# Batch one's front reworked, decays announced by halves, loads reordered: a gated SSM with a quantised FFN on one core

## The reference, cut to what matters

```
# Mamba-like mixer on ctx, gated by layernorm(x)
xin   = in_proj_w @ ctx ; xc = causal depthwise conv, 4 taps ; u = silu(xc + conv_b)     # 256 channels
dt, Bm, Cm = x_proj_w @ u                                      # 8 + 16 + 16 rows
delta = softplus(dt_proj_w @ dt + dt_proj_b) ; A = -exp(A_log)
state = state * exp(delta * A) + (delta * u) * Bm              # scan over 256 tokens, 16 states a channel
y = (sum_n state * Cm + D * u) * silu(layernorm(x))
x = x + tanh(g_xattn) * y
# FFN on layernorm(x): act_quant to 8 bits, ternary weights, gate/up 256 -> 1024,
# silu(gate) * up, Walsh-Hadamard transform, act_quant, ternary down 1024 -> 256
x = x + tanh(g_ffn) * ffn(layernorm(x))
```

## Time and profile before

| | before |
|---|---|
| median of three runs | 223.75 us |
| the profiled execution, its own time | 223.4 us |
| its span, first to last instruction | 221.6 us |
| DVE busy | 188.3 us (85%), 292 instructions |
| ACT busy | 172.8 us (78%), 302 instructions |
| PE busy | 167.9 us (76%), 1216 matmuls |
| POOL busy | 148.5 us (67%), 247 instructions |
| ACT table loads | 14 |
| granted TensorE clock, mean | 0.937 |
| first scan starts | 28.55 us |
| last product with C ends | 185.06 us |

### The profile page before, as it was taken

One profiled execution on the slowest core, in us unless ns is written; L12 is line 12 of the kernel. 1 busy time (PEld: TensorE's weight loads), 2 busy tenths in 40 slices (PEclk: granted clock), 3 DMA queues, 4 the chain that ended last, 5 costly groups with the idle time before them and its releaser, 6 DMA issues.

```text
span 221.6 us, 3745 instructions
## 1 busy us (share of the span) xinstructions
PE 167.9 (76%) x1216; PEld 136.7 (62%) x1216; DVE 188.3 (85%) x292; ACT 172.8 (78%) x302; POOL 148.5 (67%) x247
## 2 busy tenths in 40 slices
PE   2757475997897994979867968988587598677873
PEld 1535354796695984748757864877484487544751
DVE  3462889597999999999999899999979996889983
ACT  0699997799899989799879895999497630985373
POOL 1103039969787989999999999999995299510000
PEclk9965587579999999999999999999999999999999
DMA  4994000000000000000000000000000000000001
...
DMA packets 8148, 6.33 MB, mean 29 GB/s; under 512 B 2202, under 2 KB 7874, under 8 KB 8130
## 3 DMA queue, kind: packets, MB, share of 16 engines
...
...
## 4 chain that ended last, share of the span: by engine, by line
POOL 25%; DVE 11%; PE 11%; ACT 8%; issue 4%; POOLq 0%; DVEq 0%; ACTq 0%
POOL driveT L1413 7%; POOL wnat L1479 7%; POOL wnat L1478 7%; PE GP L601 2%; DVE wnat L1789 2%; ACT L1242 2%; PE PY L483 2%; PE BC L422 1%; DVE wnat L1792 1%; DVE wnat L1730 1%; DVE prod L1686 1%; DVE state L1609 1%; PE UP L422 1%; ACT xn L1163 1%; DVE wnat L1778 1%
## 5 line engine op out<-in xcount | busy, mean ns | idle before, releaser
L1413 POOL TENSOR_SCALAR driveT<-duT,BT 128x256 f32<-128x256 f32 x120 | 58.4, 506 | 14.6 <-ACT duT L1071 11.9
L1054 ACT ACTIVATE decay<-delta,zero_c,aneg 128x255 f32<-128x255 f32 x128 | 65.0, 588 | 0.1
L1686 DVE TENSOR_TENSOR prod<-state,BC 128x1024 f32<-128x1024 f32 x32 | 38.5, 1202 | 3.2 <-PE BC L467 2.7
L1609 DVE TENSOR_TENSOR_SCAN state<-decay,BC 128x512 f32<-128x512 f32 x30 | 36.4, 1212 | 2.0 <-ACT decay L1054 1.2
L1609 DVE TENSOR_TENSOR_SCAN state<-decay,UP 128x512 f32<-128x512 f32 x30 | 35.9, 1198 | 0.0
L483 PE MATMUL PY<-id,prod 128*128 128x128 f32 x256 | 33.0, 273 | 0.8 <-DVE prod L1686 0.5
L483 PEld LDWEIGHTS PY<-id,prod 128*128 128x128 f32 x256 | 28.7, 140 | 1.8 <-issue 0.8
L1478 POOL TENSOR_TENSOR wnat<-wnat 128x512 f32<-128x512 f32 x18 | 22.9, 1271 | 8.0 <-DVE wnat L1730 7.2
L422 PE MATMUL BC<-id,driveT 128*128 128x128 f32 x120 | 19.4, 286 | 8.2 <-POOL driveT L1413 4.4
L1479 POOL TENSOR_TENSOR wnat<-wnat 128x512 f32<-128x512 f32 x18 | 22.9, 1272 | 0.0
L422 PEld LDWEIGHTS BC<-id,driveT 128*128 128x128 f32 x120 | 14.4, 148 | 11.9 <-issue 5.5
...
## 6 DMA issues: line engine op xcount, KB each, us to landing
...
```

The lines of the kernel that those rows point to most:

```text
L1054: last = nc.scalar.activation(decay[:, m % RING, h, n, 1:L], delta[:, b % 2, h, 1:L], ACT.Exp, bias=zero_c[:], scale=aneg[:, h, NB * j + n ...
L1413: last = nc.gpsimd.tensor_scalar(driveT[:, m % RING, c, n], duT[:, b % 2, c], BT[:, b % 2, c, NB * j + n:NB * j + n + 1], 1.0, ALU.mult, A ...
L1609: nc.vector.tensor_tensor_scan(state[:, g % STATES, h].rearrange("p n l -> p (n l)"), decay[:, g % RING, h].rearrange("p n l -> p (n l)"), ...
L1686: nc.vector.tensor_tensor(prod[:, g % RING].rearrange("p h n l -> p h (n l)"), state[:, g % STATES].rearrange("p h n l -> p h (n l)"), PC. ...
```

## The change

1. **Loads.** The DMAs of `conv_b`, `dt_proj_w`, `dt_proj_b` and `D` move from SP's queue to ACT's (ACT issues 9 instead of 5 before it computes). On SP the rest moves up, and `x` (1 MB) is loaded ahead of the gate weights (1 MB).
2. **Early table.** `setup_loads` on ACT ends with a load of the silu set. The load at L994 and the `for_silu()` behind `first_tap` are gone.
3. **Bias in silu.** `first_tap` is a Copy with a scale; `conv_b` is added by the silu of batch 0, which becomes one activation for each half.
4. **Softplus in pieces.** `softplus(n)` is cut into `spread(n)` (Abs, and Relu from batch 1 on) and `softplus(n)` (Exp, Ln). For batch 0 DVE does the Relu (`first_relu`), and subtracts before the Ln is there (`first_rest`), so that one addition is left behind it (`first_delta`).
5. **Halved decays.** `decays(m)` becomes `decays(m, h)`, each with its own count; `scan(m, h)` waits for its half alone, and a half of a ring slot is written again once that half was scanned.
6. **New order** of the calls on PE, ACT, POOL and DVE, in the whole program.

```diff
@@ softplus_tail
-                    eng.wait_ge(act_decay, STEPS * (n - 1))
+                    eng.wait_ge(act_decay, HALF * STEPS * (n - 1))
@@ sync
-            sp.dma_start(cb[:], conv_b...)
             sp.dma_start(xpw[:], x_proj_w).then_inc(ld_small, 16)
-            sp.wait_ge(zeroed, 1)
-            sp.dma_start(dtw[:, :, DT0:DT0 + DR], dt_proj_w...)
-            for dst, src in ((dtb, dt_proj_b), (dskip, D)): sp.dma_start(dst[:], ...)
             sp.dma_start(ctxs[:, 1:B]...).then_inc(ld_ctx, 16)
+            sp.dma_start(xs[:]..., tiles(x)).then_inc(ld_x, 16)
             sp.dma_start(wnat[:, 0]..., w_gate...).then_inc(ld_w[0], 16)
-            sp.dma_start(xs[:]..., tiles(x)).then_inc(ld_x, 16)
@@ dt_proj
                 elif n == 1:
                     pe.wait_ge(act_spread, 1)
+                    pe.wait_ge(dve_relu, 1)
@@ scalar: setup_loads, first_tap
+                act.dma_start(cb[:], conv_b...) ; act.wait_ge(zeroed, 1) ; act.dma_start(dtw..., dt_proj_w...)
                 ... gates, gates, alog ...
+                act.dma_start(dtb ...) ; act.dma_start(dskip ...)
+                nc.scalar.preload_act_table_set("silu_and_others")
-                act.wait_ge(ld_cb, 16)
-                    last = nc.scalar.activation(conv[:, h], bank4[...], ACT.Identity, bias=cb[:, h:h + 1],
+                    last = nc.scalar.activation(conv[:, h], bank4[...], ACT.Copy,
                                                 scale=cw[:, h, DC - 1:DC])
@@ decays
-            def decays(m):
+            def decays(m, h):
                 if m >= RING:
-                    act.wait_ge(dve_scan, HALF * (m - RING + 1))
-                for h in range(HALF):
-                    for n in range(NB):
+                    act.wait_ge(dve_scan, HALF * (m - RING) + h + 1)
+                for n in range(NB):
@@ silu_u(0)
-                    nc.scalar.activation(u[:, 0], conv[:], ACT.Silu, bias=zero_c[:]).then_inc(act_u, 1)
+                    act.wait_ge(ld_cb, 16)
+                    for h in range(HALF):
+                        last = nc.scalar.activation(u[:, 0, h], conv[:, h], ACT.Silu, bias=cb[:, h:h + 1])
+                    last.then_inc(act_u, 1)
@@ spread, softplus
+            def spread(n):
                 act.wait_ge(pe_draw, n + 1)
                 ...
-                    nc.scalar.activation(spr[:, h], v, ACT.Relu, bias=dtb[:, h:h + 1])
+                    if n >= 1:
+                        nc.scalar.activation(spr[:, h], v, ACT.Relu, bias=dtb[:, h:h + 1])
                     last = nc.scalar.activation(spa[:, h], v, ACT.Abs, bias=dtb[:, h:h + 1])
                 last.then_inc(act_spread, 1)
+            def softplus(n): ... Exp, Ln as before
@@ vector
-                dve.wait_ge(act_decay, g + 1)
+                dve.wait_ge(act_decay, HALF * g + h + 1)
+            def first_relu():
+                dve.wait_ge(act_spread, 1)
+                dve.wait_ge(ld_conv, 16 * 2)
+                for h in range(HALF):
+                    last = nc.vector.tensor_scalar(spr[:, h], dt_bank(0)[:, L * h:L * (h + 1)], dtb[:, h:h + 1], 0.0,
+                                                   ALU.add, ALU.max)
+                last.then_inc(dve_relu, 1)
+            def first_rest():       # spm = (1 + spe) - 1 - spe on act_sp_link, then:
+                link(nc.vector.tensor_tensor(spm[:], spr[:], spm[:], ALU.subtract))
+            def first_delta():
+                dve.wait_ge(act_sp, 1)
+                nc.vector.tensor_tensor(delta[:, 0], spl[:], spm[:], ALU.add).then_inc(delta_ready, 1)
+                du_of(0, dve, nc.vector)
@@ scalar, the list of calls, its beginning now
             setup_loads() first_tap() tanh_gates() silu_u(0) xpw_out() dtw_out() for_exp() dt_rows(0)
             high_pieces(0) weight_abs(0) spread(0) inw_out() exp_A() softplus(0) copy_B(0) copy_BT(0)
             first_rstd() ctx_out() weight_abs(1) copy_B(1) decays(0, 0) decays(0, 1) decays(1, 0) decays(1, 1)
             copy_duT(0) for_silu() silu_u(1) silu_z(0) for_exp() decays(2, 0) dt_rows(1) copy_BT(1)
             high_pieces(1) decays(2, 1) spread(1) decays(3, 0) decays(3, 1) softplus(1) decays(4, 0) ...
```

497 lines of the change are left out of this document (267 added, 230 removed).

## The result

| | before | changed |
|---|---|---|
| median | 223.67 us (4 runs) | 226.65 us (225.87 to 228.56, 4 runs) |
| the profiled execution, its own time | 223.4 us | 225.87 us |
| its span | 221.6 us | 224.1 us |
| first decay | 26.45 us | 26.57 us |
| first scan | 28.55 us | 27.70 us |

What follows compares the result with a forecast made beforehand. Front bound by ACT, middle by DVE with POOL close behind, tail by a barely touched chain. 223.4 - 1.9 (front) - 1.0 (middle) = 220.5 us, with the median 0.35 above: 220.9 us, range 217.7 to 224.8.

Steps and rivals of the forecast that it cites:

- Loads, "Zero": Load order: new order and queues cost nothing; small loads took 2.7 us to land, alog needed at 8.5 us.
- which fits: ACT's start: some 4.5 us of issuing plus one table load get done before 7.46 us.
- both orders serve: Large loads: x has slack until 19.7 us, gate weights wanted at 15.7 us, so either may go first.
- The middle, "It just fits. I take 1.0 us": POOL's drives(21) ends at 125.6 us, needed at 126.7; 1.0 us gained from DVE's waits, ends 0 and 4.5.
- so it keeps the 1.9 us: Middle: DVE does the same work from times_C(4) on, so the 1.9 us gained by then stays.
- Rival (b): PE, step to batch 1: PE stays at half clock, front's gain lost, middle gives 0.5; 223.2 us, chance 0.22.
- Front: ACT up to first decay: 26.1 us against 26.45; first scan 27.1, times_C(4) 52.1 against 54.05.
- Halved decays: First scan waits for two activations, not four: 1.0 us saved; later in the run little.
- copy_duT(1): Copy that lets POOL start its chain: moved ahead of silu_z(1), to 60.2 us, 1.6 us earlier.
- Tail: End of the kernel, bound by a chain the change barely touches: zero gain, 34.6 us as before.
- Rival (c): POOL, split(3): waits for ACT's raw copy until 100 us, drives(21) ends at 132.6; total 226.8 us, chance 0.08.
- Rival (a): Middle, DVE and POOL: 4 or more of the 6.8 us of DVE idle time go; 217.7 us, chance 0.20.

Runs made afterwards that it cites:

- a_old: Changed kernel with all loads as in the kernel before, early table kept; 224.13 us, ratio 1.0013 to the kernel before.
- best2: Changed front up to times_C(6) with the loads of the kernel before, then the old order, decays halved; 222.05 us, ratio 0.9920 to the kernel before.
- best2_again: best2 unaltered, measured again; 222.25 us, ratio 0.9929 to the kernel before.
- a_old_fix: a_old with inter_out ahead of second_norm on ACT for both tiles and hadamard_mm(1,1) ahead of drive_rows(28,0) on PE; 222.99 us.
- a_small: Changed kernel with its small loads back on SP, x still ahead of the gate weights; 225.70 us, ratio 1.0117 to the kernel before.
- best1: h_front with the small loads back on SP, x still ahead of the gate weights; 224.56 us, ratio 1.0039 to the kernel before.
- h_front: Changed kernel, its loads included, up to times_C(6), then the order of the kernel before, decays halved; 226.28 us, ratio 1.0085 to the kernel before.
- h_rest: halves with the changed kernel's order from times_C(6) on, old front and loads; 226.08 us, ratio 1.0083 to the kernel before.
- halves: Kernel before with decays in halves and spread apart from softplus, nothing else moved; 223.15 us, ratio 0.9983 to the kernel before.
- segD: halves with the changed order from times_C(24) on; 225.58 us, ratio 1.0033 to the kernel before.
- after_again: Changed kernel unaltered, measured again; 226.73 us, ratio 1.0143 to the kernel before.

## Why the prediction was wrong

**Loads, "Zero": the first step that failed.** What I asked of it was that `alog` be there at 8.5 us, from a row in which a small load took 2.7 us. That row was taken where no large load was on the way. In the changed kernel `x` was issued at 2.64 us and landed at 11.1, and the loads that ACT issued from 2.80 us on landed at 8.3 and 10.1 (the gates) and 11.8 us (`alog`): `silu_u(0)` started at 12.01, 13.55, 13.78 and 15.21 us in four executions of kernels with these loads and this ACT list, and at 10.64 to 10.86 in those with the small loads on SP. The first scan of the four is at 27.70, 29.25, 29.49 and 30.92, mean 29.34; with all loads as before (a_old, best2, best2_again, a_old_fix) it is at 26.92, 27.21, 26.93 and 26.64. The step also took ACT's issuing at 4.5 us, "which fits"; it lasted until 6.65, and the table load behind it ended at 7.96, past the 7.46 at which PE was ready. In the profile of the changed kernel x_dbl(0) starts at 13.31 us, behind `silu_u(0)`, where I had 12.2.

The Trainium skill, "DMA: Bandwidth & Descriptors", section "Issuing engines are not separate DMA queues", says that DMAs started by different engines run on the same 16 and interleave; the rows are in line with that (2.7 us to 7.9 us). They do not single it out: `conv_b` and `dt_proj_w` now also stand ahead of `alog` on ACT's own queue (q10 of the profile, whose packets rose from 976 to 2064), and in the seven kernels with the early table and the small loads on SP `alog` took 4.7 to 6.5 us although the DMA engines moved under 30 GB/s. No run parts these causes.

And "both orders serve" was wrong too: put behind `x`, the gate weights come 2 us after `weight_abs(0)` wants them (2.11 us in a_small, 1.99 in best1). In the changed kernel this does not show, since ACT, late by `alog`, comes to `weight_abs(0)` only at 16.79 us; the second lateness appears when the first is mended.

Size: 2.6 us by a_old. Undone one after the other, the small loads on ACT give 1.0 (changed kernel to a_small) and x ahead of the gate weights 1.6 (a_small to a_old); on the old order 1.7 and 2.5 (h_front, best1, best2). The larger of these, the order of the large loads, is clear of the intervals both times; the small loads' part is not clear in either (0.6 and 1.0 by the ratios). On the kernel before the loads alone cost 2.4.

**The middle, "It just fits. I take 1.0 us": the second.** drives(21) ended at about 127.0 us, half of the block at 125.22, not 125.6; POOL had reached split(3) at 94.41 where I had counted 93, the same 1.4 us. But the drives were not what DVE met first. I had priced POOL's chain against the scan that needs it, and not what stands behind an instruction that waits for POOL: on ACT `inter_out` behind `second_norm`, on PE `hadamard` behind `drive_rows`, on DVE the scan behind `absmax2`. Price: 2.1 us by a_old against best2, and 2.9 by h_rest against `halves`. That much is shown. How it divides is shown less well: three lines that undo these heads of line give back 1.1 on a_old and 0.7 on the changed kernel, both within overlapping intervals, and two of them on segD give back nothing that the ratios show. The rest is open: a_old_fix's wait of 2.10 us holds POOL's late drives(21) and the new place of C_rows(20), and a kernel with C_rows(20) directly behind `drive_rows(21,0)` was not run. The premise "so it keeps the 1.9 us" was too strong as well: see the leads of best2 above.

**The clock as an amplifier.** Rival (b) had placed it at batch 1, with PE idle from 28.8 to 32.6 us. In the profiled execution PE worked until 31.25 and stood 2.04 us, x_dbl(1) ran at full clock (1.11 us, 2.04 before), and half clock came only from 40 to 47 us and cost little (times_C(1) at 40.42, within the forecast's 39.7 to 42.3). In a_old's profiled execution the rival's mechanism is there, for some 1.4 us. Later the fall came where PE had just waited, and made a Hadamard product of 1.95 us one of 3.42. The other execution (after_again) had the same waits of PE and not the fall there, and its stretch from times_C(4) to `last_residual` is 1.9 us shorter. That the clock is worth anything in the medians was not shown. The Trainium skill, "TensorE: Matmul & The Clock Gate", Part 1, has an idle array fall to half clock. The waits of 2.10, 1.78 and 2.62 us ahead of the three falls behind 54 us agree, but a wait alone does not settle it: PE stood 2.04 us (until 33.29) and 1.72 us (until 155.87) in the same execution, and 1.78 and 2.33 us at the two `hadamard` places of after_again, with the clock at 1.00 behind each.

**Front.** First decay 26.57 (forecast 26.1), first scan 27.70 (27.1), times_C(4) 52.59 (52.1). The terms were right in kind: the table loads of 1.28 us without a drain, the pieces of the silu, x_dbl(0) and dt_proj(0). That the sum came out within 0.5 us is in part luck: `silu_u(0)` was 1.1 us late by `alog`, and the sum was too high by 0.7 to 1.0 us, for with all loads as before the first decay is at 25.1 to 25.4 (forecast 26.1). The first scan of these kernels, 26.6 to 27.2, meets the forecast's 27.1 by luck too: there DVE is late instead, since `x` lands at 17.5 us. **Halved decays:** 1.0 forecast, 0.92 measured. **copy_duT(1):** 60.2 forecast, 59.53. **Tail:** unchanged, right. **Rival (c)** did not occur: split(3) starts at 94.41 us with no wait, ACT's raw copy being there. **Rival (a)** assumed that the freed waits add up; they did not.

**The sum again**, by medians: before 223.9, front and halves with the old loads and order -1.7 (best2_again), order +2.1 (a_old against best2), loads +2.6 (after_again against a_old): 226.9, measured 226.73. This sum must close to within the 0.2 us between best2 and best2_again, since a_old stands in it with both signs; it divides the difference and does not prove it. I had -1.9, -1.0 and 0.
